# Layer 0 of a two-layer gated cross-attention block: the 64-row left-over tiles of both token halves set side by side in the array, and VectorE's order of work changed

## The reference, cut to what matters

```python
def fp4_quant_dequant(x):
    xb = x.reshape(shape[:-1] + (shape[-1] // 16, 16))
    scale = jnp.max(jnp.abs(xb), axis=-1, keepdims=True) / 6.0
    scale = jnp.maximum(scale, jnp.float32(1e-12))
    xn = xb / scale
    idx = jnp.searchsorted(_MID, jnp.abs(xn))
    q = _GRID[idx] * jnp.sign(xn) * scale
def _L0_xattn_ref(q, k, v):          # a decaying sum over tokens
    r = 0.9 * r + k_t * v_t
    return q * r
def _L0_ffn_ref(x, w_gate, w_up, w_down):
    gate = fp4_linear(x, w_gate)     # 256 -> 704
    y = fp4_linear(x, w_up)          # 256 -> 704
    h = jax.nn.silu(gate) * y
    return fp4_linear(h, w_down)     # 704 -> 256
x = x + tanh(g_xattn[0]) * _L0_xattn_ref(_layernorm(x), ctx, ctx)
x = x + tanh(g_ffn[0]) * _L0_ffn_ref(_layernorm(x), w_gate, w_up, w_down)
# layer 1: softmax attention with 16 heads, then a feed-forward of 1024 with block rounding
```

## Time and profile before

| | |
|---|---|
| median of 3 runs | 823.93 us (823.91 to 826.77) |
| profiled execution, its own time | 823.79 us |
| span of its records | 821.7 us |
| TensorE busy | 704.8 us, 86% |
| VectorE busy | 691.7 us, 84% |
| ScalarE, GpSimd busy | 486.3 us (59%), 431.6 us (53%) |
| TensorE's granted clock, mean | 0.937 |
| layer 0 | to about 350 us, attention to about 665, feed-forward to the end |

### The profile page before, as it was taken

How to read it: one execution, slowest core, us unless ns; L and a number is a source line. 1 busy time by engine, 2 the same in 40 slices (tenths; PEclk the granted TensorE clock), 3 DMA queues, 4 the chain that set the end, 5 groups by cost and what they waited for, 6 DMA issues and landing times.

```text
span 821.7 us, 16554 instructions
## 1 busy us (share of the span) xinstructions
PE 704.8 (86%) x5075; PEld 517.6 (63%) x5090; DVE 691.7 (84%) x1230; ACT 486.3 (59%) x955; POOL 431.6 (53%) x331
## 2 busy tenths in 40 slices
PE   2365999999999998689999999999999876787785
PEld 1254888888888886566666666666666433455454
DVE  6856888888888878878999999998998649999995
ACT  3343455454555442428878887788878684656653
POOL 3623656646566555745444455555443516666553
PEclk9776999999999999889999999999999796989898
DMA  8710000000000000001000000000001000100011
GB/s 275 231 46 0 1 1 1 0 0 0 0 0 1 1 0 2 1 13 41 2 3 2 1 1 1 1 2 1 1 1 53 2 1 0 37 28 26 27 39 52
DMA packets 17719, 18.35 MB, mean 22 GB/s; under 512 B 1670, under 2 KB 16912, under 8 KB 17680
## 3 DMA queue, kind: packets, MB, share of 16 engines
q1 hardware_dynamic: 17084, 17.66, 6.6%
q10 hardware_dynamic: 596, 0.20, 0.1%
HBM read 13.39 MB, written 4.19 MB: 21 GB/s over the span
## 4 chain that ended last, share of the span: by engine, by line
PE 57%; DVE 20%; issue 9%; ACT 5%; POOL 3%; DMA 3%; DVEq 1%; SPq 1%; POOLq 0%; ACTq 0%
PE ps_o L540 9%; PE a_ps_pv L635 7%; PE a_ps_t L579 7%; PE a_ps_s L620 6%; PE a_ps_m L599 5%; DVE f_ps_small L1607 4%; PE ps_gu L504 4%; PE ps_gu L506 4%; PE ps_gu L505 4%; DVE f_hcode L1623 4%; PE a_ps_t L599 3%; DMA ctx<-in_ctx 2%; DVE maxima L1522 2%; PE a_ps_pv L643 1%; ACT stack_t L934 1%
## 5 line engine op out<-in xcount | busy, mean ns | idle before, releaser
L943 ACT ACTIVATE probs<-a_ps_s 128x512 f32<-128x512 f32 x256 | 148.1, 602 | 31.2 <-PE a_ps_s L620 26.6
L1522 DVE TENSOR_REDUCE maxima<-a_ps_m 128x2 f32<-128x512 f32 x160 | 102.8, 683 | 11.1 <-PE a_ps_m L599 10.9
L620 PE MATMUL a_ps_s<-stack_t 64*128 64x256 f32 x512 | 102.3, 315 | 3.9 <-ACT probs L943 1.7
L1165 POOL TENSOR_TENSOR stack<-roped,stack 128x512 f32<-128x512 f32 x32 | 42.8, 1338 | 109.5 <-DVE stack L1512 108.0
L540 PE MATMUL ps_o<-w2t,hqt 128*128 128x256 f32 (+1 forms) x384 | 99.1, 392 | 1.3 <-ACT hqt L871 0.7
L504 PE MATMUL ps_gu<-w1h,yth 128*128 128x352 f32 x256 | 86.9, 340 | 4.5 <-DVE h L1335 4.5
L934 ACT CAST stack_t<-a_ps_t 128x512 fp32r<-128x512 f32 x128 | 71.8, 585 | 31.1 <-PE a_ps_t L579 31.1
L635 PE MATMUL a_ps_pv<-probs,v_aug 128*32 128x256 f32 x1024 | 84.4, 402 | 3.0 <-ACT probs L943 2.9
L579 PE MATMUL a_ps_t<-idf,stack 128*128 128x128 f32 x512 | 76.8, 291 | 8.9 <-POOL stack L1165 5.1
L505 PE MATMUL ps_gu<-w1l,yth 128*128 128x352 f32 x256 | 83.2, 325 | 0.0
L506 PE MATMUL ps_gu<-w1h,ytl 128*128 128x352 f32 x256 | 83.1, 325 | 0.0
(11 more groups left out here) (181 smaller groups left out, 1702.7 us busy)
## 6 DMA issues: line engine op xcount, KB each, us to landing
xres<-in_x SPq DMA_DIRECT2D x16, 256.0 KB, 3.2
ctx<-in_ctx SPq DMA_DIRECT2D x16, 256.0 KB, 3.9
out_x<-f_y SPq DMA_DIRECT2D x16, 256.0 KB, 2.1
w1a_raw<-in_w_gate_up SPq DMA_DIRECT2D x1, 1024.0 KB, 5.8
w_raw<-in_w_fc SPq DMA_DIRECT2D x1, 1024.0 KB, 5.5
w_raw<-in_w_proj SPq DMA_DIRECT2D x1, 1024.0 KB, 4.8
w_raw<-in_w_down SPq DMA_DIRECT2D x1, 704.0 KB, 9.3
stack_t<-neg_max_t SPq DMA_DIRECT2D x32, 8.0 KB
```

The lines of the kernel that those rows point to most:

```text
L620: ins = nc.tensor.matmul(a_ps_s[:, half, n, :], a_stack_t[b.par][rows, 1, pair, kc * P:(kc + 1) * P], a_stack_t[b.par][rows, 0, pair, :], ...
L943: nc.scalar.activation(a_probs[:, u % 8], a_ps_s[:, u % 2], ACT.Exp).then_inc(a_exp, 1)
L1522: nc.vector.tensor_reduce(a_maxima[:, b.par, c, 4 * quad + half:4 * quad + half + 3:2], max_bank(m), X, ALU.max).then_inc(a_v_max, 1)
```

## The change

On TensorE the left-over tiles of both token halves are turned together in group 1, as two ordinary matmuls against the identity that write partitions 0 to 63 and 64 to 127 of one PSUM bank, and go to hqt[:, 1, 2] in one copy. The down weights of the left-over tile are laid into both partition halves too. Groups 1 and 3 multiply only their two full tiles; the two left-over matmuls come last, one after the other in the queue, in opposite 64-row halves of the array (l0_down_last_tile). The odd token half adds up in bank 3 of ps_gu instead of ps_o, except in the last batch. So group 2 waits for product 3 of the next batch, which reads that bank, and slice u=1 of the batch after waits for the sum into xres.

On VectorE the maxima and scale of y are taken for the next batch between product 0 and 1, no more one batch ahead at the end of the body; hcode goes ahead of product 0; y is rounded before product 3; the maximum over h comes right behind product 3, ahead of both statistics; the sum into xres is made of two instructions. GpSimd makes ys behind hq and hs before the layer norm steps, ScalarE makes ymag behind silu 2 and hmag before y's norm.

```diff
+HIDDEN_TILES = ((0, 1, 2), (3, 4, 5))
...
+        def l0_out_bank(b, c):
+            return ps_gu[:, 3, 0:D] if c and b.shifted(1) else ps_o[:, c, :]
...
@@ l0_gate_up
+                    if u == 1 and b.shifted(-2):
+                        pe.wait_ge(v_out, b.shifted(-2).count(C, C))
...
@@ l0_turn_hidden
+                for n, k in enumerate(HIDDEN_TILES[g % 2]):
+                    into = bank[:, n * P:(n + 1) * P]
+                    if k < KH0 - 1:
+                        ins = nc.tensor.transpose(into, hq[:, c * I0 + k * P:c * I0 + (k + 1) * P], idf[:, :])
+                    elif c == 0:
+                        for half in range(C):
+                            left_over = hq[:, half * I0 + k * P:half * I0 + I0]
+                            ins = nc.tensor.matmul(into[half * LAST0:(half + 1) * LAST0, :], left_over, idf[:, :],
+                                                   start=True, stop=True)
...
+            def l0_down_last_tile(b, c):
+                rows = slice(c * LAST0, (c + 1) * LAST0)
+                nc.tensor.matmul(l0_out_bank(b, c), hqt[rows, 1, 2, :], w2t[rows, KH0 - 1, :],
+                                 start=False, stop=True).then_inc(t_o, 1)
...
@@ l0_down
-                    pe.wait_ge(v_out, b.shifted(-1).count(1, 1))
-                for n in range(KH0 // 2):
+                    pe.wait_ge(v_out, b.shifted(-1).count(C, 1))
+                if g == 2 and b.shifted(1):
+                    pe.wait_ge(v_mul, b.shifted(1).count(4, 4))
...
+                    if k < KH0 - 1:
+                        ins = nc.tensor.matmul(l0_out_bank(b, c), hqt[:, g, n, :], w2t[:, k, :], start=k == 0, stop=False)
+                ins.then_inc(t_down, 1)
+                if not b.shifted(1) and g % 2:
+                    l0_down_last_tile(b, c)
+                if b.shifted(1) and g == 3:
+                    l0_down_last_tile(b, 0)
+                    l0_down_last_tile(b, 1)
...
@@ VectorE, l0_add_ffn
-                dve.wait_ge(t_o, b.count(4, 4))
-                nc.vector.scalar_tensor_tensor(tiles(xres, b), ps_o[:, :, :], gates[:, 2:3], tiles(xres, b),
-                                               ALU.mult, ALU.add).then_inc(v_out, 1)
+                for c in range(C):
+                    dve.wait_ge(t_o, b.count(C, c + 1 if b.shifted(1) else C))
+                    nc.vector.scalar_tensor_tensor(tiles(xres, b)[:, c, :], l0_out_bank(b, c), gates[:, 2:3],
+                                                   tiles(xres, b)[:, c, :], ALU.mult, ALU.add).then_inc(v_out, 1)
@@ VectorE, l0_body
                 if prv:
                     l0_hidden_up(prv)
+                    l0_hidden_codes(prv)
                 l0_multiply(b, 0)
-                if prv:
-                    l0_hidden_codes(prv)
+                l0_y_scale(nxt)
                 l0_multiply(b, 1)
...
                 l0_multiply(b, 2)
-                if b.shifted(4):
-                    l0_x_stats(b.shifted(4))
+                l0_y_round(nxt)
                 l0_multiply(b, 3)
-                l0_y_round(nxt)
-                if nxt2:
-                    l0_y_stats(nxt2)
                 l0_hidden_scale(b)
...
+                if b.shifted(4):
+                    l0_x_stats(b.shifted(4))
+                if nxt2:
+                    l0_y_stats(nxt2)
                 l0_y_low(nxt)
-                if nxt2:
-                    l0_y_scale(nxt2)
                 if prv:
                     l0_add_ffn(prv)
```

More of the change, by code:

```diff
@@ L445, in turn_w2 @@
                     kk, c = 2 * k + m // 2, m % 2
-                    rows = P if kk < KH0 - 1 else LAST0
                     at = c * I0 + kk * P
-                    ins = nc.tensor.transpose(bank[0:rows, m * P:(m + 1) * P], w_raw[W2][:, at:at + rows], idf[:, :])
+                    into = bank[:, m * P:(m + 1) * P]
+                    if kk < KH0 - 1:
+                        ins = nc.tensor.transpose(into, w_raw[W2][:, at:at + P], idf[:, :])
+                    else:
+                        for rows in (slice(0, LAST0), slice(LAST0, 2 * LAST0)):
+                            ins = nc.tensor.matmul(into[rows, :], w_raw[W2][:, at:at + LAST0], idf[:, :], start=True, stop=True)
                 ins.then_inc(t_w2, 1)
@@ L519, in l0_turn_hidden @@
                 bank = (ps_ta, ps_tb)[g % 2]
-                for n in range(KH0 // 2):
-                    k = first_k + n
-                    rows = P if k < KH0 - 1 else LAST0
-                    ins = nc.tensor.transpose(bank[0:rows, n * P:(n + 1) * P],
-                                              hq[:, c * I0 + k * P:c * I0 + k * P + rows], idf[:, :])
+                for n, k in enumerate(HIDDEN_TILES[g % 2]):
[7 more added lines that the diff above has]
+                                                   start=True, stop=True)
                 ins.then_inc(t_ht, 1)
+            def l0_down_last_tile(b, c):
+                rows = slice(c * LAST0, (c + 1) * LAST0)
+                nc.tensor.matmul(l0_out_bank(b, c), hqt[rows, 1, 2, :], w2t[rows, KH0 - 1, :],
+                                 start=False, stop=True).then_inc(t_o, 1)
             def l0_down(b, g):
-                c, first_k = g // 2, (g % 2) * (KH0 // 2)
+                c = g // 2
                 if g:
@@ L533, in l0_down @@
                 if g == 0 and b.shifted(-1):
-                    pe.wait_ge(v_out, b.shifted(-1).count(1, 1))
-                for n in range(KH0 // 2):
+                    pe.wait_ge(v_out, b.shifted(-1).count(C, 1))
+                if g == 2 and b.shifted(1):
+                    pe.wait_ge(v_mul, b.shifted(1).count(4, 4))
+                for n, k in enumerate(HIDDEN_TILES[g % 2]):
                     if g == 0 and n == 1:
                         pe.wait_ge(a_ht, b.count(4, 1))
-                    k = first_k + n
-                    rows = P if k < KH0 - 1 else LAST0
-                    ins = nc.tensor.matmul(ps_o[:, c, :], hqt[0:rows, g, n, :], w2t[0:rows, k, :],
-                                           start=k == 0, stop=k == KH0 - 1)
-                ins.then_inc(t_o, 1)
+                    if k < KH0 - 1:
[6 more added lines that the diff above has]
+                    l0_down_last_tile(b, 1)
             def l0_hidden_out(b, nxt):
@@ L771, in _ @@
             l0_turn_hidden(last, 1)
+            pe.wait_ge(v_out, last.shifted(-1).count(C, C))
             at_scores_for_max(first, 0)
@@ L813, in w2_out @@
                 bank = (ps_ta, ps_tb)[k % 2]
-                for m in range(2):
-                    rows = P if 2 * k + m < KH0 - 1 else LAST0
-                    ins = nc.scalar.copy(w2t[0:rows, 2 * k + m, :], bank[0:rows, m * D:(m + 1) * D])
-                ins.then_inc(a_w2, 1)
+                nc.scalar.copy(w2t[:, 2 * k:2 * k + 2, :].rearrange("p k n -> p (k n)"), bank[:, :]).then_inc(a_w2, 1)
             def w34_out(k):
@@ L872, in l0_hidden_out @@
                     nc.scalar.copy(hqt[:, 0, 1:3].rearrange("p a b -> p (a b)"), bank[:, P:3 * P]).then_inc(a_ht, 1)
-                elif g % 2 == 0:
-                    nc.scalar.copy(hqt[:, g].rearrange("p a b -> p (a b)"), bank[:, 0:3 * P]).then_inc(a_ht, 1)
-                else:
-                    nc.scalar.copy(hqt[0:LAST0, g, 2, :], bank[0:LAST0, 2 * P:3 * P])
-                    nc.scalar.copy(hqt[:, g, 0:2].rearrange("p a b -> p (a b)"), bank[:, 0:2 * P]).then_inc(a_ht, 1)
+                else:
+                    n = 2 if g == 3 else 3
+                    nc.scalar.copy(hqt[:, g, 0:n].rearrange("p a b -> p (a b)"), bank[:, 0:n * P]).then_inc(a_ht, 1)
             def l0_y_magic(b):
@@ L1242, in _ @@
             l0_y_quantised(first)
-            l0_y_scaled(second)
             v_aug_rows = a_v_aug[:, :, :, :, :].rearrange("p a c h s -> p (a c h) s")
@@ L1675, in _ @@
             l0_y_low(first)
-            l0_y_scale(second)
             over_batches(dve, l0_body, L0_AHEAD, L0_BEHIND)
```

21 lines of the change are left out of this document (11 added, 10 removed).

## The result

The changed kernel takes 828.78 us (median of 8 runs, 825.27 to 831.17), the kernel before 824.38 (8 runs beside it, 822.68 to 826.77): a ratio of 1.005, 95% interval 1.003 to 1.0069. It is slower by half a per cent, +4.4 us where +4.0 was forecast. The profiled executions took 823.8 and 827.2 us; the spans are 821.7 and 825.0.

The account below looks back on a forecast made before the run. TensorE bounds before at 17.02 us a batch; afterwards a ring over VectorE, GpSimd and ScalarE, 17.45. 12 periods x 0.43 = 5.2, less 1.5, plus 0.3 = +4.0 on 823.79: 827.8 us, range 815 to 833.

Parts of the forecast that it names:

- the ring: Chain over VectorE, GpSimd and ScalarE closing once per batch of layer 0: summed 17.51, taken as 17.45 us.
- the old ring: The same chain in the order before the change: 16.6 us a batch, under TensorE's 17.02.
- Steps 1, 2 and 7: Product 1 to product 3, 3.30 us; y's rounding before product 3, 0.4 more; reciprocal to next product, 0.27.
- Step 6: From hq on GpSimd to the reciprocal of y, with the scale over y waiting for hq: 2.66 us.
- Rival A: Scale slips past hq or product 1 is not late; TensorE's 16.14 holds: 812 us, half 817; chance 0.21 with Rival D.
- Rival B: The ring holds but nothing collides at y's rounding before product 3: 16.9 us a batch, 821.3 us; chance 0.17.
- Rival C: y's roundings held, hup delays the layer norm's last GpSimd step, silu 0 and product 0 late: 833 us; chance 0.15.
- Rival D: 64-row pairs not side by side: TensorE's period 16.7, forecast unchanged; 818 us under Rival A; chance 0.21 together.
- TensorE's own saving: TensorE's period alone, per batch of layer 0, falls from 17.02 to 16.14 us.
- The head: First batches, up to the first down product: 1.5 us saved (ends 0 and 2.5).
- The last two batches: The ring replaces shorter periods there and the roundings leave the way: 0.3 us lost (ends -1 and +1).
- What would show it: Signs: scale 1.6 us ending with hq, u=3 idle 0.5 to 1.2, last groups 2.8, periods 17.3 to 17.6 us.

Follow-up runs that it names:

- e4: Changed kernel with maximum, scale and reciprocal over y moved behind product 1 on VectorE; ratio to the kernel before 1.0065.
- e11: Changed kernel with all batches written out, x_mix of the next but one batch moved ahead of product 1; ratio to the kernel before 1.0028.
- e5: Changed kernel with GpSimd's sum into xres moved behind y's quantised values; ratio to the kernel before 1.0031.
- e3: Changed kernel without the scale over y from the second batch on (output differs); ratio to the kernel before 0.9945.
- e6: Changed kernel without the layer norm's shift product on GpSimd after the first batches (output differs); ratio to the kernel before 1.0068.
- e9: e8 with both last 64-row tiles taken from the same array half (output differs); ratio to the kernel before 0.9968.
- e8: Changed TensorE code with the old order on VectorE, ScalarE and GpSimd, all layer 0 batches written out; ratio to the kernel before 0.9925.
- e10: e8 without the left-over tiles' transposes after the first batch (output differs); ratio to the kernel before 0.9913.

## Why the prediction came out, and where its steps were wrong

- **What bounds, and the ring's length: right.** 17.51 was summed and 17.45 taken; measured are 17.24 in written-out batches and 17.67 in the loop, 17.52 on average over twelve. (The seven steps as printed add up to 17.52. Two more sums are off: 163.97 to 167.74 is 3.77 and not 3.7, which makes the old ring 16.66; and 16.14 + 0.43 is 16.57, not 16.7. Neither moves the forecast.) The rows that the sum stood on were read at 154 to 168 us, inside the loop, and carried its surcharge with them without my knowing. Twelve periods cost 5.9 us more, 5.2 forecast.
- **Steps 1, 2 and 7: right sum, wrong route.** "product 1 to product 3 ... 3.30 us" and "0.4 us more" were steps of a way over slice u=3 and silu 3. What bound was reciprocal to ys 0.44, to ymag 1.09, to yup 0.66, to ycode 1.16, to product 3 0.61: 3.96 us. Mine, 0.27 + 3.30 + 0.4, is 3.97. Two ways met in product 3, and I priced the wrong one (e4, e11). Its length over silu 3 was right, 3.26 us from product 1, but product 3 comes 3.69 us after product 1, because ycode holds it. The 0.4 that I put on top for yup (measured 0.43, e5) fills just this difference. That the two sums agree to a hundredth is luck; the forecast of the time rests on it.
- **Step 6, hq to the reciprocal: right, 2.66 forecast and measured.** But its cause is double: without the scale, ys still stands behind hq (e3), so 0.56 of it hangs on the scale and the rest on GpSimd's queue.
- **Rival A was mispriced.** "Without the wait the way from hcode to product 1 is ... 1.8 instead of 3.1 us, the ring 16.1": e4 made product 1 free and e3 took the wait away, and the rings were 17.21 and 16.68. It had no way to 812 us in this order, since ys stays behind hq.
- **Rival B** fell with the collision, which is there. **Rival C**: its hold is there (shift 1.51 to 1.69 us), its condition too (the shift ends 1.68 us after hup has begun, 111.84 for 110.16), y's norm is late by it, and it costs nothing (e6), because product 0 waits for hcode anyway. **Rival D**: side by side (e9).
- **TensorE's own saving: 0.88 forecast, about 0.6 measured** (17.0 to 16.42, e8). In a written-out batch of before and of e8: down group 1 and the input transposes take 2.08 and 1.40 us, -0.68 where -0.77 was said; the last hidden transposes -0.10 for -0.11; groups 2 and 3 are 2.88 and 2.88, the 0 forecast. The rest is the left-over pair, 0.87 to 1.06 us from the first hidden transpose to the first down product, costed at nothing. The copy that was to cover it covers about half; e10 shows that it cost no time all the same, because yq holds TensorE at 16.42.
- **The head: -1.5 forecast (ends 0 and -2.5), -2.8 measured, of which -1.6 between the first two maxima. The last two batches: +0.3 (ends -1 and +1), +1.5 measured.** In the second the mistake is one term: the period from batch 13 to 14 was 15.28 us before and is the ring's 16.81 now. The head's miss (-1.3) and that of the last two batches (+1.2) cancel by chance, and the periods' 0.7 is left: +4.7 where the layer ends, +4.0 forecast.
- **What would show it**: the scale at about 1.6 us ending with hq, idle before u=3 of 0.5 to 1.2, the groups with the pair within 2.9, the periods, the maximum right behind product 3, all seen. The wait before u=3 misled me as to its meaning: in e4 it is nearly gone and the batch is as long as before. It is a consequence of the ring and not a link of it.

## What to carry to other kernels

When a step is moved behind a long instruction of another engine, close every ring that passes through that engine's queue, not only the one through the wait that you see: here ys stood behind hq whether or not VectorE's scale did. Where two ways meet in one instruction, price both to their ends; the visible idle of the scarce engine may lie on the shorter. And a saving on the bounding engine is worth taking alone before it is joined to a new order: here it was 0.8% by itself, and in the ring 0.26 us of it a batch survived. How much more it can give is asked by taking something away: e8's TensorE looked fully busy, and e10 gained nothing.
